# Layer 3 of a graph kernel: rows stored unnormalised, the edge-attribute product made one layer earlier, the penalty row loaded, a bias add on GpSimd

## The reference, cut to what matters

```python
x = _layernorm(x + _L0(x, src, dst, ...))                 # attention, two rounds
x = _layernorm(x + _L1(x, edge_index, W, b))              # mean of W x[src] over the edges of dst
# _L2, the third layer:
combined = concatenate([x[dst], edge_attr], axis=-1)      # 128 + 64 features
messages = relu(combined @ W1 + b1) @ W2 + b2
agg_sum  = segment_sum(messages, dst);  agg_mean = agg_sum / max(count, 1)
agg_max  = segment_max(messages, dst)                     # 0 where there is no edge
x = _layernorm(x + agg_mean @ Wm + bm + agg_max @ Wx + bx + agg_sum @ Ws + bs)
# _L3, the fourth: h = x @ W; attention over the edges of dst, leaky_relu, softmax, sum
x = _layernorm(x + _L3(...))
```

## Time and profile before

| | us |
|---|---|
| median of 3 runs | 2331.03 (2330.08 to 2334.55) |
| the profiled execution | 2329.25 |
| its span in the profile | 2327.5 |
| busy in the span | PE 1815.2, PEld 1208.7, DVE 1689.1, ACT 1082.4, POOL 1146.8 |
| stages e, f, g, h, read from the timeline | 1147 to 1406, to 1772, to 2030, to 2327.5 |

### The profile page before, as it was taken

One profiled execution on the slowest core, in us unless ns is written; L12 is line 12 of the kernel. 1 busy time (PEld: TensorE's weight loads), 2 busy tenths in 40 slices (PEclk: granted clock), 3 DMA queues, 4 the chain that ended last, 5 costly groups with the idle time before them and its releaser, 6 DMA issues. The chain is left out here.

```text
span 2327.5 us, 31509 instructions
## 1 busy us (share of the span) xinstructions
PE 1815.2 (78%) x7816; PEld 1208.7 (52%) x7816; DVE 1689.1 (73%) x6584; ACT 1082.4 (47%) x3027; POOL 1146.8 (49%) x1193
## 2 busy tenths in 40 slices
PE   1999988995677886577566667999896999778982
PEld 1988887884532232466456554666562222245551
DVE  5765555557978883799678885999794666688772
ACT  0333322230966665255355554666565555433331
POOL 5777777760037777000377750000003777547776
PEclk9776666666898776555577887999996555566555
DMA  4655555540258675244497762323525999723440
GB/s 98 199 179 158 159 152 159 160 125 1 71 182 265 195 199 150 83 148 150 131 243 212 214 187 89 102 92 102 135 89 182 361 340 316 261 59 101 142 131 22
DMA packets 260073, 369.15 MB, mean 159 GB/s; under 512 B 94880, under 2 KB 110898, under 8 KB 259636
## 3 DMA queue, kind: packets, MB, share of 16 engines
q1 hardware_dynamic: 208956, 283.27, 38.6%
q0 software_dynamic: 37632, 67.06, 11.2%
q10 hardware_dynamic: 13304, 16.80, 2.1%
HBM read 223.76 MB, written 147.05 MB: 159 GB/s over the span
## 5 line engine op out<-in xcount | busy, mean ns | idle before, releaser
L688 POOL DMA_INDIRECT ring<-x_t,idx x280 | 266.9, 953 | 685.2 <-SPq L317 600.5
L750 ACT ACTIVATE outr<-z,rn 128x128 f32<-128x128 f32 x784 | 322.6, 483 | 306.7 <-DMA out_dram<-outr,idx 122.3
L688 POOL DMA_INDIRECT ring<-in_x_dram,idx x392 | 376.7, 961 | 136.6 <-issue 118.1
L688 POOL DMA_INDIRECT ring<-hidden_e,idx x196 | 197.5, 1008 | 195.4 <-DVE idx L1618 135.7
L694 POOL DMA_INDIRECT out_dram<-outr,idx x196 | 194.3, 991 | 103.2 <-issue 57.9
L2147 PE MATMUL bank<-DB,z 20*128 20x512 f32 x196 | 201.4, 1129 | 21.6 <-DVE outr L1593 7.1
L704 DVE BATCH_NORM_STATS2 stats<-z 128x6 f32<-128x128 f32 x784 | 170.9, 281 | 5.1
L1172 DVE BATCH_NORM_STATS2 stats<-ring 128x6 f32<-128x128 f32 x196 | 42.7, 280 | 178.4 <-DMA ring<-in_x_dram,idx 171.1
L1109 ACT ACTIVATE msg<-bank 128x512 f32<-128x512 f32 x98 | 58.5, 597 | 194.7 <-PE bank L1041 193.2
L1067 PEld LDWEIGHTS bank<-bT,msg 128*128 128x128 f32 x784 | 136.5, 261 | 1.0 <-ACT msg L1109 0.9
L1067 PE MATMUL bank<-bT,msg 128*128 128x4 f32 x784 | 135.4, 296 | 0.7 <-ACT msg L1109 0.7
(11 more groups left out here) (432 smaller groups left out, 4737.1 us busy)
## 6 DMA issues: line engine op xcount, KB each, us to landing
hT<-in_x_dram SPq DMA_DIRECT2D x194, 256.0 KB
x_t<-outr SPq DMA_DIRECT2D x147, 256.0 KB
ring<-x_t SPq DMA_DIRECT2D x147, 256.0 KB
xsrc_e<-ring SPq DMA_DIRECT2D x49, 256.0 KB, 2.4
xd_e<-ring ACTq DMA_DIRECT2D x49, 256.0 KB
ring<-xsrc_e SPq DMA_DIRECT2D x49, 256.0 KB
x_t<-xT SPq DMA_DIRECT2D x49, 256.0 KB
ring<-xd_e SPq DMA_DIRECT2D x49, 256.0 KB
```

Of the source, the lines that this page charges most:

```text
L688: nc.gpsimd.indirect_dma_start(to(c), None, table, bass.IndirectOffsetOnAxis(ap=idx[:, kind, (g + 1) * GT + c:(g + 1) * GT + c + 1].bitcas ...
L750: ins = nc.scalar.activation(to[:, k, :], frm[:, k, :], ACT.Identity, bias=sc[:, k, 1:2], scale=sc[:, k, 0:1])
```

## The change

1. **Stage f stores its rows without the norm.** The centring is folded into the weights: `centred` subtracts from each row of Mm, Ms and Mx its mean, in stage a, and the bias used is the centred one. Stage f has no statistics, root, reciprocal, shift or norm any more: `residual` writes `outr`, which is stored. The scale 1/sqrt(mean of squares + eps) is found by `squares` on ScalarE (4 activations with an accumulator output per tile) in f for a node's own rows and in g for the gathered rows; `roots` and `rates` in g turn them into rates, which multiply the dot products. In h `alpha` is multiplied by `src_rate`, and `residual` becomes four instructions that scale by `own_rate`. Each gather in g also waits for the squares of four tiles earlier.
2. **The attribute part is made in stage e.** TensorE multiplies M1b with the turned attributes (`attributes`, bank 7), ScalarE adds m1 and writes it, and 256 KB (`attrT_e`) are stored per tile where 128 KB (`eaT_e`) were. In f, M1a's product goes to one of two banks alone, VectorE adds the loaded part (`add`), and ScalarE's relu reads the sum.
3. **The penalty row is loaded**: it is made once in the preparation and loaded per tile (128 KB, in packets of 512 bytes).
4. **GpSimd makes the node columns plus bias** in f, where it had nothing to do.
5. The last root of the edge rates, which nothing uses now, is left out; some semaphores are renamed.

```diff
@@ e_tensor
-                need(pe, "e_eaT", g - 1)
+                need(pe, "e_copied", g)
                 for c in range(GT):
-                    ins = nc.tensor.transpose(bank[6 + s][0:EF, c * P:(c + 1) * P], e_ea[:, j, c, :], ident[:])
-                ins.then_inc(S("e_eatr"), 1)
+                    ins = nc.tensor.transpose(bank[6][0:EF, c * P:(c + 1) * P], e_ea[:, j, c, :], ident[:])
+                ins.then_inc(S("e_turned"), 1)
+            def attributes(i, j):
+                g = RING * i + j
+                need(pe, "e_copied", g + 1)
+                need(pe, "e_add", g)
+                nc.tensor.matmul(bank[7][:], M1b[:], e_eaT[j], start=True, stop=True).then_inc(S("e_amm"), 1)
-            pipeline(pe, [(0, turn), (1, project), (1, edges), (3, back)])
+            pipeline(pe, [(0, turn), (2, attributes), (1, project), (1, edges), (3, back)])
@@ e_scalar
+            def attributes(i, j):
...
+                nc.scalar.activation(e_attr[j], bank[7][:], ACT.Identity, bias=m1c[:]).then_inc(S("e_add"), 1)
-            pipeline(a, [(1, edges), (2, step), (4, back)])
+            pipeline(a, [(1, edges), (2, attributes), (2, step), (4, back)])
@@ f_sync
-                count(sp, "f_m1", i, j, RING)
-                sp.dma_start(f_ea[:, j], eaT_e[g]).then_inc(S(f"f_xs{j}"), 16)
+                count(sp, "f_add", i, j, RING)
+                sp.dma_start(f_attr[:, j], attrT_e[g]).then_inc(S(f"f_xs{j}"), 16)
+                count(sp, "f_max", i, j, RING)
+                sp.dma_start(f_pen[:, j].rearrange("p (q c) -> p q c", c=CH),
+                             pen_d[g * GE:(g + 1) * GE].rearrange("(q c) -> q c", c=CH)[::-1, :].partition_broadcast(P)) \
+                    .then_inc(S(f"f_xs{j}"), 16)
-                count(sp, "f_row", i, j)
+                count(sp, "f_z", i, j)
-            pipeline(sp, [(-3, load), (3, store)], [skip, masks, skip])
+            pipeline(sp, [(-3, load), (2, store)], [skip, masks, skip])
@@ f_tensor
-                nc.tensor.matmul(bank[2][:], M1a[:], X2T[:, j, :], start=True, stop=False)
-                nc.tensor.matmul(bank[2][:], M1b[:], f_ea[:, j], start=False, stop=True).then_inc(S("f_m1"), 1)
+                nc.tensor.matmul(f_first[j % 2][:], M1a[:], X2T[:, j, :], start=True, stop=True).then_inc(S("f_m1"), 1)
@@ f_scalar
-                nc.scalar.activation(hT[:, s, 0, :], bank[2][:], ACT.Relu, bias=m1c[:]).then_inc(S("f_relu"), 1)
+                nc.scalar.activation(hT[:, s, 0, :], hT[:, s, 2, :], ACT.Relu).then_inc(S("f_relu"), 1)
+            def squares(i, j):
+                g = NG - 1 - (RING * i + j)
+                count(a, "f_z", i, j)
+                count(a, "f_square", i, j, 1)
+                for k in range(GT):
+                    ins = nc.scalar.activation(squared[k], outr[:, j, k, :], ACT.Square,
+                                               accum_out=own_rate[:, g * GT + k:g * GT + k + 1])
+                ins.then_inc(S("f_square"), 1)
-            pipeline(a, [(-1, relu), (0, message), (3, apply), (0, columns), (2, means), (2, root)])
+            pipeline(a, [(-1, relu), (0, message), (2, means), (3, squares)])
@@ f_pool (new)
+                nc.gpsimd.tensor_scalar(aT[:, s, :], X2T[:, j, :], m3c[:], None, ALU.add).then_inc(S("f_xb"), 1)
@@ f_vector
-                v.tensor_scalar(neg[:, j % 2, :], m, -1.0, -FAR, ALU.add, ALU.mult).then_inc(S("f_neg"), 1)
+            def add(i, j):
+                s = j % 2
+                count(v, "f_m1", i, j)
+                count(v, "f_relu", i, j, 2)
+                v.tensor_tensor(hT[:, s, 2, :], f_first[s][:], f_attr[:, j], ALU.add).then_inc(S("f_add"), 1)
-                v.tensor_tensor_scan(MX[:, s, ::-1], neg[:, s, :], hT[:, s, 1, ::-1], ini, ALU.add, ALU.max) \
+                v.tensor_tensor_scan(MX[:, s, ::-1], f_pen[:, j, :], hT[:, s, 1, ::-1], ini, ALU.add, ALU.max) \
-            pipeline(v, [(3, scale), (-2, spread), (0, penalty), (0, totals), (2, residual), (2, norm_stats(v, "f")),
-                         (2, norm_var(v, "f"))])
+            pipeline(v, [(-2, spread), (-1, add), (0, totals), (2, residual)])
@@ g_pool, g_vector, g_scalar
+                need(pool, "g_square", g + 1 - RING)
+                    c.do(v.reciprocal(rate[:, t0:t1], rate[:, t0:t1]))
+                    c.hold()
+                    c.do(v.tensor_tensor(dot, dot, rate[:, t0:t1], ALU.mult))
+            def squares(g):
+                gathered(a, "g", g, GT * 16)
+                need(a, "g_square", g)
+                for k in range(GT):
+                    t = g * GT + k
+                    ins = nc.scalar.activation(squared[k], g_rows(g)[:, k, :], ACT.Square, accum_out=src_rate[:, t:t + 1])
+                ins.then_inc(S("g_square"), 1)
...
             for q in range(QC, NQD):
+                if q % 2 and q >= 3:
+                    squares((q - 3) // 2)
+                if q == NQD - 7:
+                    roots(0, GM)
@@ h_vector
-                v.tensor_tensor(z[:, j % 2], h_rows[j][:].rearrange("p (t f) -> p t f", f=F), rload[:, j], ALU.add) \
+                for k in range(GT):
+                    t = (NG - 1 - (RING * i + j)) * GT + k
+                    ins = v.scalar_tensor_tensor(z[:, j % 2, k, :], rload[:, j, k, :], own_rate[:, t:t + 1],
+                                                 h_rows[j][:, k * F:(k + 1) * F], ALU.mult, ALU.add)
```

More of the change, by code:

```diff
@@ L1219, in a_vector, with centred, step @@
             build(1)
+            def centred(w):
+                def step():
+                    c.link(v.tensor_reduce(wmean[:, 0:1], w, X, ALU.add))
+                    c.link(v.tensor_scalar(wmean[:, 0:1], wmean[:, 0:1], -1.0 / F, None, ALU.mult))
+                    c.link(v.tensor_scalar(w, w, wmean[:, 0:1], None, ALU.add))
+                return step
             between = bias_rows(v)
+            between.update({15 + n: centred(w) for n, w in enumerate((Mm_s, Ms_s, Mx_s[:]))})
             for n in range(len(EPARTS) - 1):
@@ L1278, in layer, with no_rate @@
                 return variance, rate
+            def no_rate():
+                c.link(v.memset(cov[:, :, steps - 1:steps], 0.0))
+            if not last_rate:
+                return [step for n in range(steps - 1) for step in layer(n)] + [no_rate]
             return [step for n in range(steps) for step in layer(n)]
@@ L1882, in rows @@
                 sp.dma_start(x2T_e[RING * i + j], e_xT[j]).then_inc(S(f"e_xo{j}"), 16)
-            return (-2, load), (2, edges), (5, rows)
+            return (-2, load), (3, edges), (5, rows)
         def e_vector(v):
@@ L1992, in combine @@
                 ins.then_inc(S("f_mm2"), 1)
-            pipeline(pe, [(-1, hidden), (0, message), (1, combine)])
+            pipeline(pe, [(-1, nodes), (0, message), (1, combine)])
         def f_rows(s, c):
             return bank[4 + s + 2 * (c // 2)][:, (c % 2) * 2 * F:(c % 2 + 1) * 2 * F]
+        own_rate, src_rate = dlo, shi
+        squared = [zf[:, (GT + k) * P:(GT + k + 1) * P] for k in range(GT)]
         def f_scalar(a):
@@ L2125, in summed, with rates @@
                 node_sum(v, q, go[q % OQ], bank[2 + q % 4])
+            def rates(t0, t1, root):
+                v.wait_ge(S("g_root"), root)
+                for rate, dot in ((own_rate, own4[:, t0:t1]), (src_rate, logit4[:, t0:t1, 0])):
+                    c.do(v.reciprocal(rate[:, t0:t1], rate[:, t0:t1]))
+                    c.hold()
+                    c.do(v.tensor_tensor(dot, dot, rate[:, t0:t1], ALU.mult))
             for g in range(NG):
@@ L2130, in g_vector @@
                         summed(q - 1)
+                if g == NG - 2:
+                    rates(0, GM, 1)
             summed(NQD - 1)
+            rates(GM, NT, 2)
+            c.hold()
         def turns(g):
@@ L2164, in g_scalar @@
                 node_rows(a, q, dqf[:, k % DQ, :], go[k % OQ])
+            squares(NG - 1)
+            roots(GM, NT)
         def g_sync(sp):
```

104 lines of the change are left out of this document (57 added, 47 removed), and 16 rows, old and new, of the table SHARED.

## The result

The changed kernel takes 2343.14 us (median of 6 runs, 2339.03 to 2346.16) against 2331.20 for the kernel before on the same chip (6 runs). The ratio is 1.0052, 95% interval 1.0040 to 1.0064: slower by half a per cent. The prediction was 2321, 10 us in the other direction; 2343 lies in its range, but only because the range took in rivals 1 and 2 (the forecast's own case ended at 2331). The profiled execution is the slowest of the six, 2346.16 with a span of 2344.4, so the two profiles differ by 16.9 us of span where the medians differ by 12.

The account below looks back on a forecast made before the run. TensorE and VectorE were taken as full in stage f, a closed ScalarE-VectorE loop as bounding e, GpSimd g and h. Terms +21 (e), -35 (f), +3.5 (g, h) gave -10.5 on 2331, so 2321 us; range 2311 to 2356.

Parts of the forecast that it names:

- rival 1: Stage f: GpSimd's add holds up VectorE's scans, 0.6 to 0.9 us per turn, whole about 2353; chance 0.36.
- rival 2: Stage f: partial contention of GpSimd's add with VectorE's scans, 0.1 to 0.4 per tile, 2326 to 2339; chance 0.10.
- the forecast's own case: Whole kernel: no contention of weight, g hidden, 2321 us, range 2312 to 2331; chance 0.45.
- Stage e, the activation inside the loop: Stage e: the added ScalarE activation before the root lengthens the turn from 4.90 to 5.47 us; stage +21.
- two engines are full, and a change must relieve both: Stage f before: TensorE needs 6.72 of a 6.81 us turn, VectorE's instructions follow almost without a gap.
- rival 4: Stage f: message not held behind relu, turn 5.75 us, whole 2295; chance 0.03.
- Stage f, the lock: Stage f: VectorE's add and sum and ScalarE's relu and message wait on each other; turn 6.30 us, -24.
- I take 0: Stage f: GpSimd's add, 0.55 to 0.9 us long, does not disturb VectorE's scans; cost 0.
- The mask stall: Middle of stage f: the stall at the mask load stays, three more loads queued behind it; +2 us.
- Start, last turns and drain of f: Stage f: start -2, last turns without spread and add -2, drain to g's first gather -9 us.
- g and h: Stages g and h: squares hidden under the gathers, end of g and start of h longer; together +3.5 us.
- rival 3: Stage g: ScalarE becomes the bound with an accumulator read of 0.3 us; +12, 2333; chance 0.06.

Follow-up runs that it names:

- experiment 1: Changed kernel with ScalarE's list in stage e reordered, root first, then the attribute activation, then the norm: 2314.33 us, ratio 0.9937.
- experiment 8: Kernel before, with ScalarE's copy of the turned attributes in stage e done twice, in front of the root: 2699.18 us, ratio 1.0059.
- Experiment 11: Kernel before without stage f's matmul of M1b with the attributes, its loads remaining: 2669.60 us, ratio 0.9959.
- experiment 3: Changed kernel with ScalarE's message placed before the relu in stage f: 2284.26 us, ratio 0.9804.
- experiment 2: Changed kernel with stage f's node columns made by ScalarE again and nothing on GpSimd: 2325.79 us, ratio 0.9970.
- experiment 10: Changed kernel with one more wait, so GpSimd's add in f starts after the spread scan of tile m+2: 2641.38 us, ratio 0.9855.
- experiment 7: Changed kernel with GpSimd's add in stage f done twice into the same place: 2657.47 us, ratio 0.9913.
- experiment 4: Changed kernel with the mask load in the middle of stage f cut into 14 pieces, one per turn: 2333.47 us, ratio 1.0019.

## Why the prediction was wrong, point by point

- **Stage e, the activation inside the loop:** right in place and size of a turn. Forecast 5.47 and a wait of 1.02 for the root, found 5.47 and 1.03; put at +20, the 36 intervals gave 199.4 - 176.9 = +22.5. Experiments 1 and 8 show the place in the list as the cause from both sides. Too small were the terms around it: the first twelve intervals +4.0 in place of +1, and the end of e +2.2, not counted. So +21 was +28.7.
- **Stage f, "two engines are full, and a change must relieve both":** wrong. I read TensorE's 67.19 of 68.07 us as need. Experiment 11 took a matmul out and the turn stayed; experiment 3 shows the need of the rest as 5.23, so by an estimate (5.23 + 0.86) the kernel before needed about 6.09 of 6.81. The forecast did not fall with it, since VectorE's and ScalarE's lock came out above either figure, but the price of rival 4 did: it was given 5.75 and 2295, and the run with the message first has 5.2 and 2284, with the losses of e and of the mask still in it.
- **Stage f, the lock:** right in kind, and 0.15 too long. Without GpSimd the loop takes 6.15 where I summed 6.30; the message starts 0.54 behind the relu (0.61 in the sum), the add is 0.70 (0.73), and the residual gives way after 0.65 (0.68).
- **GpSimd's add, "I take 0":** the step that failed first of all, since it decided the sign. It cost 0.39 us a tile, 17 to 18 us (experiments 2 and 10), above the 0.2 a tile that the prediction had named as its own failure. The Trainium skill, page "SBUF — State Buffer", section "Who interferes with whom", spoke for this: it says that a VectorE instruction with two SBUF inputs contends with a GpSimd one that reads SBUF. I set it aside because in the earlier trace rows GpSimd was the one that waited. The rows of experiment 7 agree with the exclusion and with its order deciding who waits: both directions are there. They differ from rival 1's price, the add's full length of 0.6 to 0.9: the add is 1.56 long and the scan loses only 0.49 less its distance. That is rival 2's 0.1 to 0.4 per tile, to which I had given 0.10, and the 2343 lies 4 us above its 2326 to 2339. The estimate of the add's length, 0.55 to 0.9 from a memset, was too short by 0.66 at least. So neither the forecast's case nor rival 1, which it had in second place, was right; that the range holds 2343 is luck, since its upper part was built on rival 1's price.
- **The mask stall, "+2":** it was +7.2, and 10 us go when the load is cut (experiment 4). More loads wait behind the mask, and by the prediction's own figures their lead fell from over 10 us to one turn of 6.3; the +2 priced the longer queue and left the shorter lead out.
- **Start, last turns and drain of f:** -2.5, -2.9 and -9.8 for -2, -2 and -9. Experiment 11 puts the absence of M1b's product from the start at -4.6; the further loads in front took part of that back (the first spread scan starts 8.9 us behind the end of e, against 5.9).
- **g and h:** +7.5 for +3.5. ScalarE has room (rival 3 did not occur). The gathers were slower by 11 ns at the median, 196 x 11 ns = 2.2 us; why was not tested. The rates' block in front of the last dot products is 2 more, and h's first eleven tiles are the rest.
- **The chances:** their parts add up to 0.36, 0.22 and 0.42, not 0.37, 0.21 and 0.42, and the terms of the forecast's own case span 2311 to 2333, not 2312 to 2331. Neither changes the forecast.

The terms against the profiled execution: e +7.7 above forecast, f's turns and start with the contention and the stall about +14 (-20.8 for -35), g and h +4, the stretch before e +1.5 (scatter, as said above): 27.4 in all, from -10.5 to +16.9. With nothing on GpSimd (experiment 2), or the activation placed as in experiment 1, the sign is the forecast one. With the add placed as in experiment 10 it should be on this chip too, since f is then as long as in experiment 2; that was not run there.

## What to carry to other kernels

Before pricing an operation that moves to another stage, write down that stage's closed loop and ask for its place in the list that lies in a wait: the same activation cost 25 us in front of a root and 1 us behind it. A busy share near 100% of TensorE is no proof that it is the bound; add up the smallest spacings of its matmuls' starts instead. Work given to an idle engine is not free by that alone: here GpSimd's add cost 0.39 us a tile where it began just ahead of a scan, and nothing where one wait had moved its start.

## What the runs showed of the hardware

- A GpSimd 128x512 f32 add of a column (SBUF to SBUF) takes 1.56 us alone, three times the memset of its size (0.525) in the earlier trace rows. It held up a VectorE scan with two SBUF inputs only where that started within about 0.49 us behind it (1.66, 1.51 and 1.28 us at distances of 0.10, 0.25 and 0.83), and it was itself held up behind a scan that went first (2.58 us).
- TensorE's busy time is no measure of its need: ten turns showed 67.19 us busy, and 54.69 with one matmul per turn less, so 1.25 a turn for a matmul that follows its like at 0.86; the same 128x512 matmul (by M2) is drawn 1.13 long in the earlier trace rows and 1.02 in run 3.
- The read of ScalarE's accumulator takes 0.18 to 0.22 us and overlaps the next square, so that the pairs are 0.30 apart.
- Two of the three chips run the kernel before in 2677 to 2682 us instead of 2331. In stage e the instructions have the same lengths there (the scan 1.246 us), with pauses of 3 to 4 us between. On one of them the change measured 0.9916 where it was 1.0052 before. What pauses there was not found; a verdict of half a per cent on one chip need not hold on another.
